# Scores of the first query tile by three split products in place of two full-precision passes, in a two-layer transformer kernel

## The reference

```
x = x + attn0(layernorm(x))      # 32 query heads, 8 key/value heads, causal
x = x + ffn0(layernorm(x))       # 64 low-rank experts, top 16
x = x + attn1(layernorm(x))      # RMS norm of q and k, ALiBi bias, causal
x = x + ffn1(layernorm(x))       # weights in NF4 code

# attention, for each sequence, key/value head and its 4 query heads
q, k, v = x @ Wq.T, x @ Wk.T, x @ Wv.T            # head width 128
scores  = q @ k.T / sqrt(128)                     # 256 x 256, masked above the diagonal
out     = softmax(scores) @ v
attn    = out @ Wo.T
```

## Time and profile before

| | us |
|---|---|
| median of three runs (lowest, highest) | 1724.79 (1724.78, 1726.33) |
| the profiled execution | 1727.61 |
| span of its instructions | 1725.9 |
| PE busy | 1688.7 |
| PEld busy | 1415.8 |
| DVE busy | 1271.5 |
| ACT busy | 902.0 |
| POOL busy | 589.7 |

### The profile page before, as it was taken

How to read it: one execution, slowest core, us unless ns; L and a number is a source line. 1 busy time by engine, 2 the same in 40 slices (tenths; PEclk the granted TensorE clock), 3 DMA queues, 4 the chain that set the end, 5 groups by cost and what they waited for, 6 DMA issues and landing times.

```text
span 1725.9 us, 28815 instructions
## 1 busy us (share of the span) xinstructions
PE 1688.7 (98%) x9088; PEld 1415.8 (82%) x9088; DVE 1271.5 (74%) x2349; ACT 902.0 (52%) x2448; POOL 589.7 (34%) x714
## 2 busy tenths in 40 slices
PE   8999999999999998999999999999999997899999
PEld 7888888888888887987888888888888886688887
DVE  5788888888888787544777787778777779655555
ACT  2666566655565645323545555554445546554443
POOL 4325344343626254232213121222212103344442
PEclk9999999999999999999999999999999999999999
DMA  4122222221312221000101001100111002022111
GB/s 153 38 68 67 73 79 61 73 84 49 97 53 87 66 89 62 1 1 31 37 25 38 30 30 30 30 30 30 30 30 30 24 5 81 24 75 61 58 52 49
DMA packets 47711, 87.78 MB, mean 51 GB/s; under 512 B 6576, under 2 KB 6576, under 8 KB 47536
## 3 DMA queue, kind: packets, MB, share of 16 engines
q1 hardware_dynamic: 47664, 87.19, 16.3%
HBM read 77.73 MB, written 9.44 MB: 51 GB/s over the span
## 4 chain that ended last, share of the span: by engine, by line
PE 58%; DVE 4%; ACT 2%; POOL 1%; issue 1%; DMA 0%; DVEq 0%; ACTq 0%; POOLq 0%
PE ring L323 11%; PE ring L325 11%; PE ring L324 11%; PE scores L323 4%; PE scores L324 4%; PE scores L325 4%; PE turned L323 3%; PE turned L324 3%; PE turned L325 3%; PE scores L745 2%; PE turned L819 2%; PE turned L785 1%; PE turned L812 1%; ACT p L845 1%; PE turned L806 0%
## 5 line engine op out<-in xcount | busy, mean ns | idle before, releaser
L323 PE MATMUL ring<-xt_hi,w_lo 128*128 128x512 f32 x640 | 253.8, 397 | 2.4 <-issue 1.4
L325 PE MATMUL ring<-xt_hi,w_hi 128*128 128x512 f32 x640 | 253.3, 396 | 0.0
L324 PE MATMUL ring<-xt_lo,w_hi 128*128 128x512 f32 x640 | 253.2, 396 | 0.0
L588 POOL TENSOR_SCALAR w_hi<-w_raw 128x512 fp32r<-128x512 f32 x96 | 66.6, 693 | 501.8 <-PE turned L806 306.6
L323 PE MATMUL ring<-wd_hi,ot_lo 128*128 128x512 f32 x512 | 207.9, 406 | 10.2 <-DVE xt_lo L508 3.8
L836 ACT CAST pt_hi<-turned 128x512 fp32r<-128x512 f32 x192 | 100.7, 594 | 197.8 <-PE turned L812 193.5
L325 PE MATMUL ring<-wd_hi,ot_hi 128*128 128x512 f32 x512 | 202.9, 396 | 0.0
L324 PE MATMUL ring<-wd_lo,ot_hi 128*128 128x512 f32 x512 | 202.8, 396 | 0.0
L564 ACT ACTIVATE lv_early<-code_early 128x512 f32<-128x512 f32 x224 | 123.1, 640 | 54.5 <-POOL code_early L555 53.1
L323 PEld LDWEIGHTS ring<-xt_hi,w_lo 128*128 128x128 f32 x640 | 120.9, 189 | 28.7 <-issue 1.7
L325 PEld LDWEIGHTS ring<-xt_hi,w_hi 128*128 128x128 f32 x640 | 120.6, 188 | 28.9
(11 more groups left out here) (250 smaller groups left out, 4382.6 us busy)
## 6 DMA issues: line engine op xcount, KB each, us to landing
w_raw<-w_attn_dram SPq DMA_DIRECT2D x96, 256.0 KB, 3.1
wd_raw<-w_dense_dram SPq DMA_DIRECT2D x64, 256.0 KB, 2.7
code_early<-codes_dram SPq DMA_DIRECT2D x28, 256.0 KB, 2.8
absmax_early<-absmax_dram SPq DMA_DIRECT2D x56, 128.0 KB, 3.0
kept_dram<-deq_early SPq DMA_DIRECT2D x28, 256.0 KB, 2.0
stage<-kept_dram SPq DMA_DIRECT2D x28, 256.0 KB, 2.7
code_late<-codes_dram SPq DMA_DIRECT2D x14, 256.0 KB, 2.7
absmax_late<-absmax_dram SPq DMA_DIRECT2D x28, 128.0 KB, 2.9
```

The lines of the kernel that those rows point to most:

```text
L323: nc.tensor.matmul(o, l_lo, r_hi, start=start, stop=False)
L324: nc.tensor.matmul(o, l_hi, r_lo, start=False, stop=False)
L325: return nc.tensor.matmul(o, l_hi, r_hi, start=False, stop=stop)
```

## The change

The scores of the first query tile are now made by `mm3` as well, from the first 128 columns of the sequence in `qt_hi`, `qt_lo`, `kt_hi` and `kt_lo`. The plain copies are no longer made. Their memory stays reserved under new names, so no other tensor moves.

```
+                        first = q_slot(of, 0)
                         for h in range(HEADS):
-                            ins = nc.tensor.matmul(scores0[:, h, :], qt_f[:, h, of, :], kt_f[:, of, :],
-                                                   start=True, stop=True)
+                            mm3(scores0[:, h, :], qt_hi[:, h, first], qt_lo[:, h, first], kt_hi[:, first], kt_lo[:, first])
...
-                        tile_b = tile.rearrange("p (b s) -> p b s", b=2)
...
                         if X == K:
-                            nc.scalar.copy(kt_f[:, 2 * half:2 * half + 2, :], tile_b[:, :, 0:P])
                             act_ring_hi(nc.scalar.copy(kt_hi[:, cols], tile))
                         else:
                             h = X - Q0
-                            nc.scalar.copy(qt_f[:, h, 2 * half:2 * half + 2, :], tile_b[:, :, 0:P])
                             act_ring_hi(nc.scalar.copy(qt_hi[:, h, cols], tile))
...
-                        nc.scalar.activation(kt_f[:, 2 * half:2 * half + 2, :],
-                                             tile.rearrange("p (b s) -> p b s", b=2)[:, :, 0:P], ACT.Identity,
-                                             scale=norm_cols[:, 2:3])
                         act_ring_hi(nc.scalar.activation(kt_hi[:, cols], tile, ACT.Identity, scale=norm_cols[:, 2:3]))
```

More of the change, by code:

```diff
@@ L600, in attention @@
             qt_lo = sb(f"qt_lo{layer}", [P, HEADS, TOK], F32R, scope)
-            qt_f = sb(f"qt_f{layer}", [P, HEADS, BATCH, P], F32, scope)
+            sb(f"after_queries{layer}", [P, HEADS, BATCH, P], F32, scope)
             kt_hi = sb(f"kt_hi{layer}", [P, TOK], F32R, scope)
             kt_lo = sb(f"kt_lo{layer}", [P, TOK], F32R, scope)
-            kt_f = sb(f"kt_f{layer}", [P, BATCH, P], F32, scope)
+            sb(f"after_key{layer}", [P, BATCH, P], F32, scope)
             v_hi = sb(f"v_hi{layer}", [P, NT, HD], F32R, scope)
```

## The result

| | before | after |
|---|---|---|
| median, us (lowest to highest) | 1724.78 (1723.94 to 1726.33) | 1748.3 (1747.54 to 1750.97) |
| profiled execution, us | 1727.61 | 1748.01 |
| span, us | 1725.9 | 1746.3 |

The ratio is 1.0137, with a 95% interval of 1.0123 to 1.015: slower by 23.6 us (21 to 26). The forecast was 1749.8 us, +25.0.

A forecast was written before the change was run, and what follows sets the result against it. TensorE, busy 98% of the time, was taken to bound the kernel: +28.4 us for added weight loads less 3.4 us of shorter waits gave +25.0, or 1749.8 us beside the median 1724.79, with a range of 1743 to 1761 us.

The forecast's parts named there:

- TensorE is the bound: Whole kernel: PE is busy 1688.7 of 1725.9 us, so a microsecond added to TensorE in a slot lengthens the kernel equally.
- The load sets the pace, at 0.111 us: First-tile scores: loading 128 weight columns takes longer than a 64 ns matmul, so narrow split products start 0.111 us apart.
- The upper bound of 0.119: First-tile scores: a 128-column split product costs at most 0.119 us, the price of a 256-column one; +34.4 us.
- Four loads more in a slot, +28.4 us: First-tile scores: 12 loads with matmuls replace 8 at 0.111 us each, 0.444 us a slot over 64 slots.
- The relief of 3.4 us: TensorE's waits: 3.0 us gained at `ot_lo` and 0.44 at `wd_lo`; range 0 to 6 us.
- eight waits on `ot_lo` at 0.38 us: Before the output projection, one wait in each first-layer group, all expected to go, gaining 3.0 us.
- The 0.4 at `wd_lo`: The single 3.1 us wait on the split output weights shrinks by 0.44 us, as one longer score step lies between.
- either covers it: At `ot_lo`: 0.5 us less ScalarE copying or PE coming 0.44 us later would each cover the 0.38 us wait.
- The chance for a clock that falls in slots: Rival, 3%: denser loads and shorter matmuls lower TensorE's granted clock in the slots, giving 1765 us or above.
- Columns alone: Rival, 6%: loads hide and moving columns set the narrow split products' pace at 0.064 us, giving 1714 us.
- Format lost below 256 columns: Rival, 8%: split products under 256 columns run like full-precision ones, adding 114 us, giving 1839 us.
- The halfway pace of 0.087: Rival, 6%: loads of the narrow split products hide in part, +9.9 us less the 3.4 of relief, giving 1731 us.

The follow-up runs named there:

- e1: Kernel before with the three split products of 128 columns added and the plain copies still made by ScalarE; ratio 1.0137, 1750.47 us beside 1726.13.
- e5: Kernel after with 64 moving columns in place of 128 in the 12 split products of a slot; ratio 1.0139 to the kernel before.
- e6: Kernel after with weights of 64 columns in place of 128 in the 12 split products of a slot; ratio 0.9932 to the kernel before, 1713.55 us.
- e3: Kernel after with only two of the three split products, low by high left out; ratio 0.9972 to the kernel before, 1721.81 us.
- e2: Kernel after with first-tile scores again in full precision, from the high parts only, plain copies still dropped; ratio 0.9964, 1720.34 us beside 1726.13 of before.
- e7: Kernel before, full precision with plain copies, with 64 moving columns in place of 128 in the first query tile's passes; ratio 1.0003.

## Why the prediction was right

- *TensorE is the bound.* Right: about 25 us of added periods turned into 23.6 us of time, and 40 us less of ScalarE (e1 against the change) into nothing that the times can tell. That ScalarE's busy time would fall by 60 us was wrong; it fell by 40.
- *The load sets the pace, at 0.111 us.* Right, and shown from both sides: halving the moving columns changes nothing (e5), halving the weight columns brings 0.061 (e6). The upper bound of 0.119 was not needed.
- *Four loads more in a slot, +28.4 us.* Right: 0.44 to 0.45 us in each slot, and taking the four away again brought 28.5 us (e3). The sign that the prediction named for it, a first part of the scores of 1.33 us, is not met as it stands: read from end to end it is 1.42, and the periods, not this distance, show the 0.44.
- *One of its two supports was unsound.* I had read the 0.11 us between the first two loads of split scores in the earlier trace rows as the length of a load. In e6 the first two loads stand 0.11 apart as well (406.96 and 407.07), though each needs only half of that. So that distance does not measure the load; what sets it is not shown. The other support, 188 against 134 ns in the earlier trace rows, was enough, and e6 bears it out.
- *The relief of 3.4 us.* It came out at about 4.6, by terms that were each somewhat off. I had counted eight waits on `ot_lo` at 0.38 us, read from one distance of starts; there were seven, and by the periods each was worth 0.45 to 0.49, so 3.0 was 3.2 to 3.4. The 0.4 at `wd_lo` is as forecast. The waits on the probabilities, which I had held to be fixed, gave 0.9. In e1, with all copies in place, they stay at 3.9, so the dropped copies shorten them and not the later TensorE. With these terms the sum is 28.4 - 4.6 = 23.8 us, against 23.6 measured and 25.0 forecast; the interval of the measurement, 21 to 26, can't tell the two sums apart. The cause at `ot_lo` I had left as "either covers it", and that is what was found: a later TensorE does it alone (e1), and so does a lighter ScalarE (e2). In the change both are there and count once.
- *The chance for a clock that falls in slots.* Not seen: over the stretches of the earlier trace rows the attention of after has a granted clock of 1.00, as before, and the dip near the end of the second is in both (0.72 over 1447 to 1453 us after, 0.68 in the earlier trace rows). Between the attentions the clock moved the profiled pair by over 3 us, which the sum had no term for.
- *The rivals.* Columns alone (1714 us) is what e6 shows for half the weights, and only there. Format lost below 256 columns (1839 us) is excluded by the 0.112 us in the timeline. The halfway pace of 0.087 is not seen either. (Its chances do not agree with each other: a third of 6% is 2%, and the closing paragraph counts 4% within 0.2%.) The 81 ns for a load with a matmul of 128 columns in the Trainium skill ("TensorE: Matmul & The Clock Gate", section "Back-to-back issue gap") doesn't hold in either of the two float32 formats: 0.111 to 0.112 us in both. The load of columns / 1.2 ns in the Trainium skill, same page, section "LDWEIGHTS (loading the stationary operand)", 107 ns for 128 columns, does fit: it is some 5 ns under the pace.

## What to carry to other kernels

Where every matmul brings its own load, count weight columns as well as moving columns. Here no product of the scores with 128 weight columns came cheaper than 0.111 us, in either format. Up to what width moving columns are free can only be estimated: 128 of them cost 0.061 us by themselves (e6) and 256 cost 0.119, and a straight line between the two reaches 0.111 at about 240. Where three split products begin to win over two full-precision passes is an estimate too, since no run has widths between. At 128 columns they lose, 3 x 0.111 = 0.33 us against 2 x 0.111 = 0.22. At full precision 512 columns take about 0.44 us (the 0.23 of a split product and the 209 ns by which the record is longer in the earlier trace rows), 0.86 ns a column, so two passes cost 0.33 us at about 195 columns. From about there on the split products should be the cheaper ones.

Work taken from an engine with idle time is worth the waits that hang on it, once, and something else may already have paid for them.

## What the runs showed that I had not expected

Dropping the copies alone brought more than forecast: 4.7 us at equal clock, where -2 to -3 was expected (e2). In a full-precision pass of 128 columns the prediction let load and columns coincide; one with 64 costs the same (e7: ratio 1.0003). Halving the weight columns of the narrow products (e6) would make them cheaper than full precision, 12 x 0.061 = 0.73 us a slot against 0.89; but a full tile then needs twice as many, so that gives a kernel nothing as it stands. And two executions of nearly the same instructions can differ by 3 us between the attentions alone, by whether two stretches run at 1.00 or at 0.91 of the clock.
